# A three-pass projection in every second late unit, two batches kept in SBUF, and the rounding constant lifted by GpSimd

## The reference

```
h   = gelu(W_sess[id]^T (x masked by channel) + b_sess[id])      # 256 x 2048
o   = (W2^T h + b2) masked by time                               # 128 x 2048
q   = fp8_e5m2(o * s_o)          s_o = 57344 / max|o| over all 32 batches
wq  = fp8_e4m3(weight * s_w)     s_w = 448 / max|weight|
out = x + (q wq^T) / s_o / s_w + bias                            # 128 x 2048
```

## Time and profile before

| | us |
|---|---|
| median of 3 runs | 832.73 (832.57 to 832.79) |
| the profiled execution | 833.1 |
| its span in the trace | 831.3 |
| TensorE busy in the span | 825.8 |
| GpSimd busy | 511.8 |
| VectorE busy | 479.5 |
| ScalarE busy | 345.9 |

### The profile page before, as it was taken

The page is one execution under the profiler, slowest core; times in us unless marked ns, Lnnn a source line. Parts: engine busy times, 40 slices in busy tenths (PEclk is TensorE's granted clock), DMA queues, the critical chain, the costliest instruction groups (busy, mean ns, idle before and its releaser), DMA issues.

```text
span 831.3 us, 10181 instructions
## 1 busy us (share of the span) xinstructions
PE 825.8 (99%) x3568; PEld 479.9 (58%) x3568; DVE 479.5 (58%) x499; ACT 345.9 (42%) x372; POOL 511.8 (62%) x238
## 2 busy tenths in 40 slices
PE   9999999999999999999999999999999999999998
PEld 5777777776767676765444444444444444444444
DVE  6989889788888888888553232323232323232322
ACT  7999999988888888973100000000000000000000
POOL 2899999899999999995983242424242423232322
PEclk9999999999999999999999999999999999999999
DMA  7988999877777877657974868686868686868682
GB/s 258 322 321 321 367 339 353 301 285 296 284 289 303 305 267 301 253 187 246 298 295 119 282 214 282 210 285 212 280 213 280 214 283 214 279 213 282 215 248 107
DMA packets 75008, 220.77 MB, mean 266 GB/s; under 512 B 37594, under 2 KB 40930, under 8 KB 55778
## 3 DMA queue, kind: packets, MB, share of 16 engines
q1 hardware_dynamic: 74080, 219.30, 74.5%
q10 hardware_dynamic: 898, 1.09, 0.4%
HBM read 143.04 MB, written 69.21 MB: 255 GB/s over the span
## 4 chain that ended last, share of the span: by engine, by line
PE 99%; issue 0%; POOL 0%; DVE 0%; ACT 0%; POOLq 0%
PE ps_h L1071 53%; PE ps_h L980 22%; PE ps_o L995 11%; PE ps_o L1011 8%; PE ps_o L1007 4%; PE ps_o L934 1%; PE ps_h L1047 0%; PE ps_o L1071 0%; PE ps_o L980 0%; PE ps_o L1065 0%; POOL time L518 0%; PE ps_o L940 0%; PE ps_h L1052 0%; DVE o_and_max L881 0%; ACT x_sb L702 0%
## 5 line engine op out<-in xcount | busy, mean ns | idle before, releaser
L1071 PE MATMUL ps_h<-wqT,x_sb 128*128 128x512 bf16 x1920 | 413.7, 378 | 0.2 <-ACT x_sb L702 0.2
L1071 PEld LDWEIGHTS ps_h<-wqT,x_sb 128*128 128x128 fp8e5 x1920 | 187.7, 98 | 224.4 <-ACT x_sb L702 0.3
L528 POOL TENSOR_TENSOR xl<-x_sb,xh 128x1024 fp32r<-128x1024 f32 x62 | 149.5, 2411 | 16.3 <-ACT xh L607 16.3
L980 PE MATMUL ps_h<-xh,whl 128*128 128x512 f32 x508 | 150.3, 417 | 0.4
L569 POOL TENSOR_TENSOR x_sb<-x_sb,bias_sb 128x2048 f32<-128x2048 f32 (+1 forms) x15 | 66.7, 4447 | 131.7 <-DMA x_sb<-in_x 131.7
L569 POOL TENSOR_TENSOR h<-h,bias_sb 128x2048 f32<-128x2048 f32 (+1 forms) x15 | 66.7, 4443 | 122.7 <-DMA h<-in_x 122.7
L881 DVE SCALAR_TENSOR_TENSOR o_and_max<-ps_h,scales,h 128x512 f32<-128x512 f32 (+1 forms) x59 | 44.0, 746 | 136.2 <-PE ps_h L1071 136.2
L881 DVE SCALAR_TENSOR_TENSOR o_and_max<-ps_h,scales,x_sb 128x512 f32<-128x512 f32 x59 | 44.2, 750 | 133.4 <-PE ps_h L1071 133.4
L980 PEld LDWEIGHTS ps_h<-xh,whl 128*128 128x128 f32 x508 | 94.2, 188 | 42.0 <-issue 21.7
L765 DVE SCALAR_TENSOR_TENSOR o_and_max<-ps_o,b_sb,steps 128x1024 f32<-128x1024 f32 (+1 forms) x65 | 82.2, 1264 | 29.0 <-PE ps_o L1011 27.1
L755 DVE TENSOR_TENSOR hl<-ps_h,hh 128x1024 fp32r<-128x1024 f32 x63 | 76.8, 1219 | 13.4 <-ACT ps_h L614 13.3
(11 more groups left out here) (101 smaller groups left out, 657.2 us busy)
## 6 DMA issues: line engine op xcount, KB each, us to landing
x_sb<-in_x SPq DMA_DIRECT2D x44, 1024.0 KB, 5.7
masked_out<-o_and_max SPq DMA_DIRECT2D x32, 1024.0 KB, 6.8
o_in<-masked_out SPq DMA_DIRECT2D x32, 1024.0 KB, 8.9
out<-o_and_max SPq DMA_DIRECT2D x27, 1024.0 KB, 5.1
wqT<-in_L_ffn_weight SPq DMA_DIRECT2D x23, 684.0 KB, 8.3
wt<-in_L_ffn_weight SPq DMA_DIRECT2D x40, 384.0 KB, 5.5
h<-in_x SPq DMA_DIRECT2D x14, 1024.0 KB, 7.2
whl<-split_w SPq DMA_DIRECT2D x18, 256.0 KB, 6.0
```

Source lines behind the costliest of these rows:

```text
L528: pool.tensor_tensor(xl[:, u % 2, :], x_cols(u), xh[:, u % 2, :].bitcast(fp32), ALU.subtract)\
L980: mm = nc.tensor.matmul(to[:, cols], whl[:, b % SLOTS_W, rows], xs[:, u % 2, cols], start=(k == 0), stop=(k == 2))
L1071: mm = nc.tensor.matmul(bank, q[:, k // 2, :, k % 2], wq[:, n, k, cols], start=(k == 0), stop=(k == KT - 1))
```

## The change

- Units 27 and 28 join SPLIT_H1. The odd units from 29 to 61 (SPLIT_BEHIND) get the three passes too: ScalarE makes the high part hh1_behind and the full gelu in PSUM, and VectorE the remainder hl1_behind, right behind `mask_o` (`split_h1_behind`). `hidden(u+1, 1)` waits for it, as it overwrites that PSUM. In these units `scan_o` comes last in VectorE's order.
- The rounding constant: ScalarE writes |w| times a scale to wc in two bytes (Abs with w_up), GpSimd bounds it below and above (`lift_constant`), VectorE computes wt times w_scale plus wc into ws in one operation (`add_round_at`), and GpSimd subtracts wc. `exponents`, `round_at` and GpSimd's addition go. A wt buffer is free after the add.
- Chunk i begins in unit i + 28; 33 chunks are done in the units, 10 afterwards, and the last loads are issued by ScalarE.
- The batches 30 and 31 (KEPT) stay in SBUF, both o and x: they are the first two of the second stage, and aren't stored or read again.

```diff
-    ROUND_AT = 1.5 * 2.0 ** 20
+    ROUND_AT = 2.0 ** 20
-    SPLIT_H1 = [u for u in range(2, 27)]
+    SPLIT_H1 = [u for u in range(2, 29)]
+    SPLIT_BEHIND = [u for u in range(29, UNITS - 2, 2)]
-    QUANT = SCANS + 2
+    QUANT = SCANS + 4
-    QUAD = 4
+    QUAD, KEPT = 4, 2
-    CHUNK_BEHIND = range(4, 12)
+    CHUNK_BEHIND = (2, 4, 5, 6, 7, 8)
...
-                if 0 <= i < CHUNKS:
+                if 0 <= i < CHUNKS and u < UNITS - 1:
                     if i >= 3:
-                        sp.wait_ge(w_scaled, i - 2)
+                        sp.wait_ge(w_added, i - 2)
                     load_chunk(i)
...
+            def lift_constant(i):
+
+                c = wc[:, i % 2, 0:chunk_cols(i)]
+                pool.wait_ge(w_raised, i + 1)
+                pool.tensor_scalar(c, c, 2.0 * E4M3_MAX * ROUND_AT, 1.5 * E4M3_MIN_NORMAL * ROUND_AT, ALU.min, ALU.max)\
+                    .then_inc(w_floored, 1)
+
             def round_chunk(i):
 
                 v, c = ws[:, i % 2, 0:chunk_cols(i)], wc[:, i % 2, 0:chunk_cols(i)]
-                pool.wait_ge(w_round_ready, i + 1)
-                pool.tensor_tensor(v, v, c, ALU.add).then_inc(w_added, 1)
                 pool.wait_ge(w_added, i + 1)
                 pool.tensor_tensor(wqT[:, CHUNK_AT[i]], v, c, ALU.subtract).then_inc(w_rounded, 1)
...
                 if 0 <= u - QUANT - 1 < EARLY_CHUNKS:
                     round_chunk(u - QUANT - 1)
+                if 0 <= u - QUANT < EARLY_CHUNKS + 1:
+                    lift_constant(u - QUANT)
...
             pool.wait_ge(bias_loaded, 16)
-            pool.wait_ge(x2_loaded[0], 16)
             add_bias(x2[0], FRONT)
-            for i in late[0:2]:
+            round_chunk(late[0])
+            lift_constant(late[1])
+            pool.wait_ge(xl_ready, UNITS)
+            add_bias(x2[1], FRONT)
+            lift_constant(late[2])
+            pool.wait_ge(q_ready, CUTS)
+            for b in range(KEPT):
+                pool.tensor_tensor(x3[:, b, :], x2[b][:, FRONT.stop:F], bias_sb[:, FRONT.stop:F], ALU.add).then_inc(x3_ready, 1)
+            for i in late[1:7]:
                 round_chunk(i)
-            pool.wait_ge(x2_loaded[1], 16)
-            add_bias(x2[1], FRONT)
-            for i in late[2:6]:
-                round_chunk(i)
+                lift_constant(i + 2)
             pool.wait_ge(x2_more_loaded[0], 16)
             add_bias(x2_more[0], FRONT)
...
+                if u in SPLIT_BEHIND:
+                    act.activation(hh1_behind[:, u % 2, :], ps_h[:, 1, :], ACT.Gelu, bias=hbias[:, 1, b:b + 1])
+                    act.activation(ps_h[:, 1, :], ps_h[:, 1, :], ACT.Gelu, bias=hbias[:, 1, b:b + 1])\
+                       .then_inc(h1_gelu, 1)
+                    return
...
-                act.activation(ws[:, i % 2, 0:chunk_cols(i)], wt[:, at:at + chunk_cols(i)], ACT.Copy, scale=w_scale)\
-                   .then_inc(w_scaled, 1)
+                act.activation(wc[:, i % 2, 0:chunk_cols(i)], wt[:, at:at + chunk_cols(i)], ACT.Abs, scale=w_up)\
+                   .then_inc(w_raised, 1)
...
+            def split_h1_behind(u):
+
+                dve.wait_ge(h1_gelu, u + 1)
+                if u == SPLIT_BEHIND[0]:
+                    dve.wait_ge(wl_later, DIRECT - UPB)
+                dve.tensor_tensor(hl1_behind[:, :], ps_h[:, 1, :], hh1_behind[:, u % 2, :].bitcast(fp32), ALU.subtract)\
+                   .then_inc(hl1_behind_ready, 1)
...
+            def add_round_at(i):
+
+                c, at = wc[:, i % 2, 0:chunk_cols(i)], i % 3 * CHUNK
+                dve.wait_ge(w_floored, i + 1)
+                dve.scalar_tensor_tensor(ws[:, i % 2, 0:chunk_cols(i)], wt[:, at:at + chunk_cols(i)], w_scale, c,
+                                         ALU.mult, ALU.add).then_inc(w_added, 1)
...
                     mask_o(u - 1, start, 0, slice(0, UNIT))
+                    if u in SPLIT_BEHIND:
+                        split_h1_behind(u)
...
-                    scan_o(u - 1, 0, slice(0, UNIT))
+                    if u not in SPLIT_BEHIND:
+                        scan_o(u - 1, 0, slice(0, UNIT))
                 if 0 <= u - QUANT - 1 < EARLY_CHUNKS + 1:
-                    exponents(u - QUANT - 1)
-                if 0 <= u - QUANT - 1 < EARLY_CHUNKS:
-                    round_at(u - QUANT - 1)
+                    add_round_at(u - QUANT - 1)
                 if u + 1 < UNITS:
                     split_h_rest(u + 1)
+                if u in SPLIT_BEHIND:
+                    scan_o(u - 1, 0, slice(0, UNIT))
...
+                    if u - 1 in SPLIT_BEHIND:
+                        pe.wait_ge(hl1_behind_ready, SPLIT_BEHIND.index(u - 1) + 1)
...
+                elif u in SPLIT_BEHIND:
+
+                    for j, (w, hs) in enumerate(((w2l1, hh1_behind[:, u % 2, :]), (w2h1, hh1_behind[:, u % 2, :]),
+                                                 (w2h1, hl1_behind))):
+                        for cols in halves:
+                            mm = nc.tensor.matmul(ps_o[:, u % 2, cols], w[:, :], hs[:, cols],
+                                                  start=False, stop=(j == 2))
```

More of the change, by code:

```diff
@@ L120, in adaln_ffn @@
         o_max = sb("o_max", [P, UNITS + 1], fp32)
-        scales = sb("scales", [P, 10], fp32)
+        scales = sb("scales", [P, 11], fp32)
         w_pmax, w_rec, w_scale, w_inv = (scales[:, k:k + 1] for k in range(4))
-        o_pmax, o_amax, o_rec, o_scale, o_inv, y_scale = (scales[:, k:k + 1] for k in range(4, 10))
+        o_pmax, o_amax, o_rec, o_scale, o_inv, y_scale, w_up = (scales[:, k:k + 1] for k in range(4, 11))
         wqT = sb("wqT", [P, WCOLS], bf16)
         x_sb = sb("x_sb", [P, 2, T], fp32)
+        raw_at = -(-nc.sbuf_base // 32) * 32
         raw = sb("raw", [P, SLOTS_W, HID], fp32)
+        assert SLOTS_W * HID == UNIT
         whl = sb("whl", [P, SLOTS_W, 2 * HID], fp32r)
@@ L299, in adaln_ffn @@
         o_row = ps_h[:, 1, 0:P]
[L301 to L307, removed]
         @block.sync
@@ L443, in _ @@
             turn(1)
[L444 to L448, removed]
+            load_x_more(1)
             for b in range(2):
@@ L475, in _ @@
                 sp.wait_ge(y_ready, QUAD * (NC - 1) + b + 1 + FREE4)
-                sp.dma_start(out[b, :, FRONT.stop:F], x3[:, b, :]).then_inc(y3_stored, 16)
+                sp.dma_start(out[batch_at(b), :, FRONT.stop:F], x3[:, b, :]).then_inc(y3_stored, 16)
             def step2(i, last):
@@ L572, in _ @@
             pool.wait_ge(bias_loaded, 16)
-            pool.wait_ge(x2_loaded[0], 16)
             add_bias(x2[0], FRONT)
-            for i in late[0:2]:
+            round_chunk(late[0])
[7 more added lines that the diff above has]
+            for i in late[1:7]:
                 round_chunk(i)
-            pool.wait_ge(x2_loaded[1], 16)
-            add_bias(x2[1], FRONT)
-            for i in late[2:6]:
-                round_chunk(i)
+                lift_constant(i + 2)
             pool.wait_ge(x2_more_loaded[0], 16)
             add_bias(x2_more[0], FRONT)
-            for i in late[6:]:
+            for i in late[7:]:
                 round_chunk(i)
+                if i + 2 < CHUNKS:
+                    lift_constant(i + 2)
             pool.wait_ge(x2_more_loaded[1], 16)
@@ L587, in _ @@
             pool.wait_ge(x3_loaded, 16)
-            for b in range(QUAD):
+            for b in range(KEPT, QUAD):
                 pool.tensor_tensor(x3[:, b, :], x3[:, b, :], bias_sb[:, FRONT.stop:F], ALU.add).then_inc(x3_ready, 1)
@@ L704, in _ @@
                    .then_inc(q_widened, 1)
[L705 to L709, removed]
+            for i in range(EARLY_CHUNKS + 1, CHUNKS - 1):
+                if i > EARLY_CHUNKS + 1:
+                    scale_chunk(i + 1)
+                if i + 3 < CHUNKS:
+                    act.wait_ge(w_added, i + 1)
                     at = i % 3 * CHUNK
@@ L796, in weight_scale @@
                 dve.wait_ge(scale_step, 1)
+                dve.tensor_scalar(w_up, w_rec, E4M3_MAX * ROUND_AT, None, ALU.mult).then_inc(w_scale_ready, 1)
                 dve.tensor_scalar(w_scale, w_rec, E4M3_MAX, None, ALU.mult).then_inc(w_scale_ready, 1)
-                dve.wait_ge(w_scale_ready, 1)
+                dve.wait_ge(w_scale_ready, 2)
                 dve.reciprocal(w_inv, w_scale).then_inc(scale_step, 1)
@@ L855, in _, with quantize_kept, quantize @@
             dve.wait_ge(scale_step, 5)
-            def quantize(r, loads, first, cols, to=q8):
-                if first:
-                    dve.wait_ge(o_in_loaded[r], loads * 16)
+            def quantize_kept(r, cols):
                 dve.sem_inc(q_turn, 1)
-                dve.tensor_scalar(to[:, r, cols], o_in[:, r, cols], o_scale, None, ALU.mult, saturate=False)\
+                dve.tensor_scalar(q8[:, r, cols], o_sb[:, r, cols], o_scale, None, ALU.mult, saturate=False)\
+                   .then_inc(q_ready, 1)
+            def quantize(r, loads, to=q8):
+                dve.wait_ge(o_in_loaded[r], loads * 16)
```

(15 more changed lines are left out.)

84 lines of the change are left out of this document (37 added, 47 removed).

## The result

The changed kernel takes 842.36 us (median of 4 runs, 842.2 to 842.58) against 832.75: the ratio is 1.0114, 95% interval 1.0102 to 1.0126. It is slower by 9.6 us where 7.3 were forecast. The spans are 840.5 and 831.3 us.

The account below looks back on a forecast made before the run. The prediction took TensorE, busy 99% of the span, as the bound. It summed -0.7 + 6.1 + 1.9 = +7.3 us, giving 840.4 us for a profiled run and a median of 840.0 us, range 829.5 to 848.

Parts of the forecast that it names:

- Units 27 and 28, -0.7: TensorE's project1 in these two units: the existing three-pass form saves 0.34 us each, -0.7 us together.
- All odd units alike: Odd units 29 to 61: each of the 17 was given the same cost, 6.25 us instead of 5.89.
- ScalarE hides the second gelu: ScalarE in the odd units: 11.2 to 11.3 us of work a pair fits within TensorE's 11.44, tight but hidden.
- The remainder behind the mask, +0.24: VectorE's remainder after mask_o delays TensorE's hidden(u+1, 1) by 0.24 us in each of 17 odd units.
- The add is held by xl, +0.46 an odd unit: VectorE's two-SBUF-input add_round_at waits for GpSimd's xl subtraction to end, delaying TensorE 0.46 us in each odd unit.
- Rival 1: add_round_at beside xl is not held, so the kernel is faster: 830.3 us; chance 0.28.
- The size of a pair, 12.14: TensorE's chain over one even and one odd unit takes 12.14 us instead of 11.78, giving +6.1 us over 17.
- The lift, 0.9: GpSimd's lift_constant, bounding the rounding constant, takes 0.9 us a chunk; anything above is paid once a pair.
- Rival 2: GpSimd's lift costs as much as a two-input operation and GpSimd is the bound: 852.8 us; chance 0.12.
- rival 3: VectorE's add slips in ahead of GpSimd's xl in most units: 832.2 us, the same as before; chance 0.10.
- The end of the units, +1.9: After the last units, GpSimd's bias for batch 30 holds add 33, delaying hl(63) and VectorE's chain: +1.9 us.
- Kept batches and late chunks, 0: Second stage: saved stores and loads gain nothing, the 10 remaining chunks cost nothing; upper bound +2 us for the chunks.

Follow-up runs that it names:

- e2: Kernel before plus only the three-pass odd units 29 to 61, remainder on VectorE behind the mask, old chunk rounding kept: 830.53 us.
- e3: Changed kernel with add_round_at reading one SBUF tensor plus a fixed number instead of wc, its rows kept apart by a gap: 831.38 us.
- e9: Kernel before plus only the three-pass odd units, with a second SBUF input given to VectorE's two-byte multiply that makes wc: 862.17 us.
- e4: Changed kernel without GpSimd's lift work: lift_constant only waits and counts, and add_round_at waits for ScalarE's Abs: 841.21 us.
- e6: Changed kernel with GpSimd's first bias (batch 30) made to wait for VectorE's add of chunk 33: 844.38 us.
- e1: Changed kernel without the three-pass form in odd units from 29 on (SPLIT_BEHIND empty), the new rounding constant kept: 835.72 us.
- e5: Changed kernel with GpSimd starting xl only after VectorE's add of that unit, in the units with chunks: 842.27 us.

## Why the prediction was right

*Units 27 and 28, -0.7.* Right. Not run alone, but the order of time has it: from hidden(28, 0) to hidden(30, 0) it is 165.47 to 176.60 in the changed kernel and 165.82 to 177.60 in the one before, 0.65 us less. The other 0.35 was gained before unit 27, and no run tells by what.

*All odd units alike.* Wrong for the first one, unit 29: it takes 183.66 - 176.60 = 7.06 us where 6.25 were forecast. ScalarE comes to it late: the first of its two gelus begins 0.67 us before the unit's first matmul (175.93) and not 1.47, and x split, xl, add and hl follow 0.8 us later. So at 183.66 the chain is at +0.16 and not at -0.3 as forecast, and the 16 pairs behind it bring it to +7.30.

*ScalarE hides the second gelu.* Right, but for unit 29: e2 and e3 carry it at 11.67 us a pair.

*The remainder behind the mask, +0.24.* Right: 0.22 in e3 and 0.14 in e2. In the changed kernel it lies inside the longer wait and isn't paid on top.

*The add is held by xl, +0.46 an odd unit.* Right, and this is what the slowdown is. Counted from the odd unit's start at 336.62 in the chain: x split at +0.36 (forecast 0.37), xl at +1.60 (1.55), add done at +4.82 (4.8), hl done at +5.95 (6.0). e3 takes the second input away and the whole loss goes; e9 puts one in elsewhere and a loss comes; e4 and e2 clear the lift, the gelu and the remainder. Rival 1 is out. The second input is enough for a hold, but not needed for one: the quantization in e6 is held with one, and its hold at 398.02, which the prediction took for a doubt, was a real one.

*The size of a pair, 12.14.* Measured 12.23, and this is the term that was most too small: 16 x 0.09 = 1.4 of the missing 2.3 us. The first odd unit's 0.8 and the 0.4 between medians and spans come to it, the 0.35 from before unit 27 stands against it, and the end of the units and the second stage, -0.3 and +0.3, cancel. I had counted semaphore and weight load once, 0.24. The chain has 0.14 for it, but after each such stall the next group of six matmuls takes 1.62 us instead of 1.39, so a stall costs 0.37 at its end.

*The lift, 0.9.* 0.848. Rival 2 is out, and rival 3 as well: xl begins 0.07 to 0.09 us after its input in the odd units and 0.2 to 0.7 in the even ones, ahead of the add in every unit.

*The end of the units, +1.9.* hl(63) ends 6.88 us after hidden(63, 0) begins (forecast 6.75, before 4.77), and the stretch from there to the first product is 1.62 us longer. The first product itself comes 8.9 us later than before (forecast about 7).

*Kept batches and late chunks, 0.* The second stage is 0.3 us longer. VectorE waits 8.3 us for the bias of x_more (before 7.8), until 426.98, and TensorE isn't held. But this was luck in part: the bias was put at 416.4 to 420.4 at its end and ends at 426.89, and that TensorE has cover for 6 us more wasn't worked out. That the kept batches gain nothing was read from the traces and not tried alone.

The medians differ by 0.4 us more than the spans; this lies outside the span and was not followed.

## What to carry to other kernels

Before an operation is moved between VectorE and GpSimd, count the SBUF tensor inputs of VectorE's and ask which GpSimd instruction runs beside it: here two inputs meant that it waited for the end of that instruction, however few the busy microseconds of either engine. With one of two tensor inputs in PSUM it wasn't held (`mask_o`, hl). One input is no safe sign: the exponents (0.94 us) and the two-byte multiply ran unhindered beside GpSimd, the quantization to fp8 did not, so look in the trace for the operation itself. Such a wait costs only where the engine's next result is on time by less than the hold (e1 against the changed kernel), so a part that looks nearly free alone, +3.0 us in e1, can be dear beside another. Here the three-pass units are worth having with the old rounding: e2, at 0.9974 of before, is the version to keep.

## What the runs showed of the hardware that was not expected

- When add and bias were issued 0.05 us apart (380.27 and 380.32 in e5), the VectorE record starts first, and still it was VectorE that waited: its add took 4.34 us and ended 0.81 us after the bias.
- An operation with two two-byte SBUF inputs took 0.95 us for 768 columns with GpSimd idle (e9, 411.79), the same with one 0.55.
- The hold goes both ways: at 386.59 GpSimd's addition took 2.61 us instead of 1.65, beside a quantization that ran from 386.43 to 387.71.
- A quantization with one tensor input was held by GpSimd: 2.31 us at 398.02 instead of 1.28.
- A stall of TensorE that ended with hl cost 0.23 us beyond its end, in the first group of six matmuls behind it (1.62 us instead of 1.39).
- GpSimd's two-byte minimum and maximum over 768 columns took 0.85 us, half of its two-input addition of 1.65.
